# A state-space layer with a routed mixture of experts: VectorE's up product and its second scan change places

## What is computed

```python
xz = rms_norm(x) @ in_proj_w ; xb, z = split(xz)
xc = silu(causal_conv4(xb) + conv_b)
dt, B, C = split(xc @ x_proj_w)
dt = softplus(dt @ dt_proj_w + dt_proj_b)
h[t] = exp(dt[t] * A) * h[t-1] + dt[t] * B[t] * xc[t]     # 512 channels x 16 states
y[t] = sum_s h[t, :, s] * C[t, s]
out = ((y + xc * D) * silu(z)) @ out_proj_w + x
...
g = x @ gate_proj[e] ; u = x @ up_proj[e]                 # for all 16 experts e
y = sum_e combine[:, e] * ((silu(g) * u) @ down_proj[e])  # combine: 4 chosen of 16, else 0
```

## Time and profile before

| | |
|---|---|
| median of three runs | 2569.0 us (2568.81 to 2570.22) |
| the profiled execution, its own time | 2567.86 us |
| its span, first to last instruction | 2566.1 us |
| granted TensorE clock, mean | 0.972 |
| TensorE busy | 2358.2 us, 92% |
| VectorE busy | 2383.7 us, 93% |
| ScalarE busy | 1624.6 us, 63% |
| GpSimd busy | 1507.3 us, 59% |
| scans (line 1140), 2 x 512 | 626.5 + 595.0 us, mean 1262 and 1203 ns |
| gate product, up product (lines 1230, 1235), 256 each | mean 676 and 663 ns |

### The profile page before, as it was taken

The page is one execution under the profiler, slowest core; times in us unless marked ns, Lnnn a source line. Parts: engine busy times, 40 slices in busy tenths (PEclk is TensorE's granted clock), DMA queues, the critical chain, the costliest instruction groups (busy, mean ns, idle before and its releaser), DMA issues.

```text
span 2566.1 us, 26884 instructions
## 1 busy us (share of the span) xinstructions
PE 2358.2 (92%) x8416; PEld 1173.7 (46%) x8416; DVE 2383.7 (93%) x3057; ACT 1624.6 (63%) x3266; POOL 1507.3 (59%) x531
## 2 busy tenths in 40 slices
PE   6556899999999999999999999999999999988998
PEld 2112354544545454454545445454544545443555
DVE  4999999999999999999999999999999999999642
ACT  6565667676766667676676757667676766655341
POOL 0554566656566666666666566666657566666522
PEclk9767899999999999999999999999999999999999
DMA  4441443545254453525345353534535353443232
GB/s 140 179 148 41 150 142 121 170 117 186 80 169 140 131 178 113 181 90 166 131 132 189 101 181 102 166 128 132 181 100 187 112 158 119 143 158 93 77 77 64
DMA packets 172922, 344.51 MB, mean 134 GB/s; under 512 B 16075, under 2 KB 81388, under 8 KB 164460
## 3 DMA queue, kind: packets, MB, share of 16 engines
q1 hardware_dynamic: 164860, 334.93, 39.4%
q0 software_dynamic: 7920, 7.87, 2.3%
HBM read 291.35 MB, written 51.38 MB: 134 GB/s over the span
## 4 chain that ended last, share of the span: by engine, by line
DVE 59%; issue 18%; PE 12%; ACT 10%; DMA 0%; POOL 0%; DVEq 0%; ACTq 0%; POOLq 0%
DVE hs L1140 27%; DVE hs L1118 14%; DVE th L1235 5%; DVE th L1230 5%; PE Gp L494 3%; ACT dA L605 3%; PE MY L512 3%; PE FP L419 3%; DVE XC L1068 2%; PE Up L502 2%; DVE SZ L1147 1%; ACT SZ L678 1%; ACT L605 1%; PE Y L528 1%; ACT L678 1%
## 5 line engine op out<-in xcount | busy, mean ns | idle before, releaser
L963 POOL TENSOR_TENSOR hs<-hs,Cb 128x2048 f32<-128x2048 f32 x256 | 1160.7, 4534 | 169.4 <-DVE hs L1118 168.8
L605 ACT ACTIVATE dA<-dtr,A 128x512 f32<-128x512 f32 x1024 | 701.4, 691 | 678.2 <-DVE hs L1140 675.7
L948 POOL TENSOR_TENSOR th<-th,cmb 128x512 f32<-128x512 f32 x256 | 337.4, 1321 | 873.1 <-DVE hs L1118 775.9
L1140 DVE TENSOR_TENSOR_SCAN hs<-dA,carry,hs 128x512 f32<-128x512 f32 x512 | 626.5, 1262 | 6.2 <-ACT dA L605 6.0
L1118 DVE TENSOR_TENSOR hs<-dxr,Bb 128x2048 f32<-128x2048 f32 (+3 forms) x483 | 616.9, 1280 | 1.8 <-PE Y L528 1.8
L1140 DVE TENSOR_TENSOR_SCAN hs<-dA,hs 128x512 f32<-128x512 f32 x512 | 595.0, 1203 | 15.1 <-ACT dA L605 14.6
L494 PE MATMUL Gp<-x2T,Wgu 128*128 128x512 f32 x1024 | 507.7, 618 | 41.2 <-DVE th L1230 39.7
L512 PE MATMUL MY<-Wdn,th 128*128 128x256 f32 x2048 | 486.0, 381 | 0.8 <-POOL th L948 0.8
L502 PE MATMUL Up<-x2T,Wgu 128*128 128x512 f32 x1024 | 483.2, 594 | 0.0
L512 PEld LDWEIGHTS MY<-Wdn,th 128*128 128x128 f32 x2048 | 383.3, 190 | 136.3 <-issue 92.4
L494 PEld LDWEIGHTS Gp<-x2T,Wgu 128*128 128x128 f32 x1024 | 175.6, 190 | 365.4 <-issue 278.0
(11 more groups left out here) (189 smaller groups left out, 1795.6 us busy)
## 6 DMA issues: line engine op xcount, KB each, us to landing
dxr<-dx_d SPq DMA_DIRECT2D x128, 512.0 KB, 7.2
cmb<-cm_d SPq DMA_DIRECT2D x256, 256.0 KB, 3.7
dtr<-dt_d SPq DMA_DIRECT2D x63, 1024.0 KB, 5.5
Wdn<-in_w_dn SPq DMA_DIRECT2D x256, 128.0 KB, 3.6
Bb<-bc_d SPq DMA_DIRECT2D x64, 256.0 KB, 3.0
Cb<-bc_d SPq DMA_DIRECT2D x64, 256.0 KB, 3.5
dt_d<-XB SPq DMA_DIRECT2D x15, 1024.0 KB, 4.3
dx_d<-DX SPq DMA_DIRECT2D x15, 1024.0 KB, 5.9
```

What stands on the lines that cost most here:

```text
L605: act.activation(dA[h % 2][:, :], dtr[:, M % 2, beta, :], ACT.Exp, scale=A[:, k:k + 1]).then_inc(s_dA, 1)
L948: pool.tensor_tensor(th[:, q % NTH, :], th[:, q % NTH, :], cmb[:, q % 2, :], ALU.mult).then_inc(m_a, 1)
L963: pool.tensor_tensor(hs[:, G % NH, :, :], hs[:, G % NH, :, :], Cb[:, s, :].unsqueeze(1).broadcast_to([P, NBETA, CH]), ALU.mult).then_inc(s ...
L1140: dve.tensor_tensor_scan(hv, dA[h % 2][:, :], hv, first, ALU.mult, ALU.add).then_inc(s_h, 1)
```

## The change

VectorE issues `scan(G, 1)` ahead of `expert_up` of the group's first expert, in every group that has both. In groups with two experts the second one's gate and up stay where they are. The computation on `ties` at the start is removed with its semaphore, and A is multiplied by the constant -1.0.

```diff
@@ prepare
                 dve.memset(picked[:, :, NE:], 1e-20)
                 dve.memset(top8[:, 1, :, :], TAKEN)
-                ties = comb[:, 16:64]
-                dve.memset(ties[:, 0:16], 3.0)
-                dve.memset(ties[:, 32:48], 8.0).then_inc(t_dve, 1)
-                dve.wait_ge(t_dve, 1)
...
-                dve.match_replace(ties[:, 16:32], top8[:, :, 0, 0:TOPK], ties[:, 0:16], TAKEN).then_inc(t_dve, 1)
-                dve.wait_ge(t_dve, 4)
-                dve.scalar_tensor_tensor(out=ties[:, 16:32], in0=ties[:, 16:32], scalar=TAKEN, in1=ties[:, 32:48], op0=ALU.is_equal, op1=ALU.mult).then_inc(t_dve, 1)
-                dve.wait_ge(t_dve, 5)
-                dve.tensor_reduce(ties[:, 0:1], ties[:, 16:32], AX.X, ALU.add).then_inc(t_dve, 1)
-                dve.wait_ge(t_dve, 6)
-                dve.tensor_scalar(ties[:, 1:2], ties[:, 0:1], -1.0, None, ALU.mult).then_inc(t_dve, 1)
-                dve.wait_ge(t_dve, 7)
                 dve.memset(XB[:, :, 0:HIST], 0.0).then_inc(w_dve, 1)
                 dve.wait_ge(w_act, 1)
-                dve.tensor_scalar(A[:, :], A[:, :], ties[:, 1:2], None, ALU.mult).then_inc(w_dve, 1)
+                dve.tensor_scalar(A[:, :], A[:, :], -1.0, None, ALU.mult).then_inc(w_dve, 1)
@@ the loop over groups, VectorE
                 if S:
                     scan(G, 0)
+                if S:
+                    scan(G, 1)
                 if done:
                     expert_up(done[0])
                 if S:
-                    scan(G, 1)
                     scan(G, 2)
                 if len(done) == 2:
                     expert_gate(done[1])
```

More of the change, by code:

```diff
@@ L209, in sandwich_kernel @@
         dt_0, dx_0, st_dt0, st_dx0, ld_half, s_u0 = (sem(k) for k in ('dt_0', 'dx_0', 'st_dt0', 'st_dx0', 'ld_half', 's_u0'))
-        x1_sum, out_sum, z_add, m_half, z_last, t_dve = (sem(k) for k in ('x1_sum', 'out_sum', 'z_add', 'm_half', 'z_last', 't_dve'))
+        x1_sum, out_sum, z_add, m_half, z_last = (sem(k) for k in ('x1_sum', 'out_sum', 'z_add', 'm_half', 'z_last'))
         block = ctx.enter_context(nc.Block())
```

## The result

| | before | after |
|---|---|---|
| median of 14 runs each, side by side | 2569.16 us (2568.14 to 2570.22) | 2574.66 us (2573.81 to 2576.31) |
| ratio, 95% interval | | 1.0022 [1.0015, 1.0030] |
| span of the profiled execution | 2566.1 us | 2572.4 us |
| granted TensorE clock, mean | 0.972 | 0.973 |
| VectorE busy / TensorE busy | 2383.7 / 2358.2 us | 2384.8 / 2368.1 us |

The change makes the kernel slower by 5.5 us. The forecast was +2.4 with "within 0.2%" (5.1 us) as the likeliest case; the time lies inside the forecast range, just past those 0.2% on the slow side.

What follows compares the result with a forecast made beforehand. The prediction took VectorE's work and waits to bound the middle and TensorE the end. Its terms, -8.3 + 5.9 + 2.0 + 2.8 = +2.4 us on 2569.0, gave 2571.4 us, range 2563.0 to 2578.0.

Steps and rivals of the forecast that it cites:

- Group 4, the gain: In group 4 VectorE's wait for n_v shrinks as the second scan ends 0.58 us earlier: 14 chunks x 0.59, -8.3 us.
- Group 13, through group 11: Group 11's later up matmul delays z2, tanh and the decay before group 13's third scan: 13 x 0.45, +5.9 us.
- Group 9, through group 7: Group 7's later up matmul brings a new wait before group 9's third scan: 6 x 0.34, +2.0 us.
- Group 5: TensorE 0.1 to 0.35 us later in groups 14 to 0, taken as absorbed, at worst 0.1 in every second chunk.
- The end: From about 2365 us, three two-expert groups start the second up matmul some 1.15 us later each: +2.8 us after gaps.
- The test products: Removing them at the start costs and gains zero, since VectorE then idles 4.88 us waiting for ScalarE.
- A: Rival: TensorE's delay is absorbed in the middle, -8.3 and the end's +2.8 stand: 2563.5 us, chance 0.15.
- B: Rival: group 11's delay passes on whole, group 13's wait grows by 1.18 instead of 0.45: 2580.9 us, chance 0.15.
- C: Rival: TensorE's clock falls behind the added pauses, +13.8 us over 13 chunks: 2585 us, chance 0.04.
- D: Rival: nothing moves, ScalarE's and TensorE's shifts cancel within 1 us: 2569 us, chance 0.04.

Runs made afterwards that it cites:

- undoing of group 11: The changed kernel with the old order kept in group 11 only: 2571.15 us, ratio 1.0008 to the kernel before.
- double dose: The changed kernel, but in group 11 the up product comes one scan later still, behind the third scan: 2594.99 us, ratio 1.0103 to the kernel before.
- the exchange alone: The changed kernel with the test products kept, the new order everywhere: 2575.16 us, ratio 1.0022 to the kernel before.
- the first filling: New order only in groups 3 and 4; in group 13 half of the next group's inputs ahead of the third scan: 2623.35 us, ratio 1.0212 to before.
- the removal alone: The kernel before with only the computation on ties (test products) removed, the old order everywhere: 2568.19 us, ratio 0.9996.
- group 4 alone: The changed kernel with the new order only in group 4, the old one elsewhere: 2562.36 us, ratio 0.9966 to the kernel before.
- all but group 7: The changed kernel with the old order kept in group 7 only: 2571.88 us, ratio 1.0012 to the kernel before.

## Why the prediction was right and where it failed

**Group 4, the gain.** Forecast 14 x 0.59 = 8.3; measured 7.90 in the 13 chunks of the middle, right link by link: in even chunks 0.12 us of the wait for n_v is left, where 0.15 was forecast. In chunk 15 the 0.7 us are there too, but by another wait and so by luck: VectorE's wait for n_v fell only from 0.70 to 0.52 us, and 0.62 us came ahead of group 4, whose gate product waited 0.29 instead of 0.91 us for tanh.

**Group 13, through group 11.** Forecast 13 x 0.45 = 5.9; measured 4.42, 0.34 per chunk. The mechanism is right, the size 0.1 too large. z2 came 0.46 us later, as forecast. What I missed is small: behind its idle time z2 took 1.98 us, without one 1.88, so 0.1 came back before tanh (0.36 later). The undoing of group 11 and the double dose show both sides of the term: 0.34 for the first, all of 1.15 for the second.

**Group 9, through group 7.** Forecast 6 x 0.34 = 2.0; measured 2.99. The wait is 0.34 us to the digit, but a wait costs more than its length: VectorE's next instruction usually starts 0.08 us before the one ahead of it ends, and a wait loses that overlap too. Per event the ledger shows 0.45; likewise 0.76 for the 0.65 in group 5. The odd chunks added 0.05 each.

**Group 5: the step that failed.** The prediction's "in groups 14 to 0 TensorE gets 0.1 to 0.35 us later, which I see absorbed, or at worst 0.1 per chunk in every second chunk" was wrong: it cost 0.76 us in each even chunk, 5.4 us, and this is the whole difference between "no change that can be told" and a slowdown. Two errors made it. I looked for TensorE's delay alone, and the place where the two engines meet had 0.36 us of room, which 0.40 us would barely have touched. But my own gain in group 4 moves VectorE 0.6 us towards TensorE at that same place. I followed the gain up to n_v and no further. Of the 5.4 us, keeping the old order in groups 14 to 0 takes 3.0 away; the other 2.5 stay as long as group 4 gains.

**The end.** Forecast +2.8. The stretch from chunk 15 to the end is +2.14; 0.73 us were gained in its groups 3 and 4, so the two-expert groups cost 2.87 (ledger of groups 11 to 14: -0.31, +1.07, +0.87, +1.18; the exchange alone repeats each within 0.01). No fall of the clock lay in these groups, neither before nor after. The rows, which answer to the earlier trace rows:

```profile
2393.73 1.89 PE L494 MATMUL Gp<-x2T,Wgu 128*128 128x512 f32 x4
2396.66 1.98 PE L502 MATMUL Up<-x2T,Wgu 128*128 128x512 f32 x4 [1.05 <-DVE th L1215]
...
2409.42 1.98 PE L502 MATMUL Up<-x2T,Wgu 128*128 128x512 f32 x4 [0.97 <-DVE th L1215]
```

In each of the three groups that the forecast named one up matmul idles about 1 us (the third, at 2374.04 us, 0.97), and TensorE sets the time there.

**The test products.** Forecast zero; measured by themselves 0.02 us at the first scan.

**The sum.** Terms as measured from chunk 2 on: -8.6 + 4.4 + 3.0 + 5.4 + 2.9 and 0.4 of small entries = 7.5, the 5.37 + 2.14 of the ledger. The profiled execution was 1.1 us ahead at chunk 2, which no edit explains (next section). The medians are 5.5 us apart.

**The rivals.** A (all absorbed): the waits contradict it. B (group 11's delay passes whole): group 13 grew by 0.34, far from 0.65; it is right only for a second dose. C (the clock): the granted clock stayed at 1.00 in the middle with pauses of up to 1.2 us, so "by these rows I add nothing" held. The rule weighed against it (the Trainium skill, page "TensorE: Matmul & The Clock Gate", part 1: a TensorE that was idle gets half its clock) does act in this kernel, but it was seen only behind longer pauses: 2.14 us in the double dose, 3.6 us in the first filling. D (nothing moves): +5.5 rules it out.

## What to carry to other kernels

A gain on one engine is a delay of every other engine against it. Follow it past the wait that it removes to the next place where the two meet, and look up the room there, which no list of waits shows: it is the distance between the end of the one and the start of the other. And where an edit stands in a loop over unlike groups, apply it only in the group where it pays: here one group of sixteen gave -7 us, all sixteen +5.5.

## What was not expected of the hardware

- **A VectorE product stood still for GpSimd, the instructions around it did not.** Beside `read_out` the product of two SBUF tensors waited until GpSimd's end (3.56 us for 1.21). In the same rows the scan at 1067.46 kept its 1.21 us with `read_out` running since 1066.54, and so did the product with Up its 0.66. Each of these two reads one input from PSUM (dA, Up) and only one from SBUF, so the page named above, which speaks of two SBUF inputs, agrees with them as well. A scan with both inputs in SBUF was not run.
- **Behind which of TensorE's pauses the clock fell.** From 290 to 2300 us, with the clock at 1.00 ahead of the pause: behind none of the 58 pauses of 0.5 to 1.2 us in the changed kernel, nor behind any in the kernel before, the longest 1.6 us; at 1.96 us (double dose) in none of 7; at 2.14 us in 2 of 6 (2.4 to 1.2 GHz for 3.4 us); at 2.81 us, once in the first filling, it fell; at 3.60 to 3.75 us in 12 of 13, for 3.4 or 6.8 us (the one at 315.60 us was spared).
- **The start is not repeatable, the middle is.** From chunk 2 to chunk 15 the ledger repeats within 0.15 us between profiles of the same order (two pairs: the changed kernel and the exchange alone, 0.02; the kernel before and the removal alone, 0.15). The way to chunk 2, where the granted clock alternates, does not: three versions with the same start as others (the exchange alone, group 4 alone, all but group 7) were 4.5 to 4.8 us ahead of before at chunk 2 in their profiled executions, the others lay between 2.1 ahead and 1.4 behind. The kernel before itself has single runs of 2563.93 and 2564.35 us beside a median of 2569.86. In chunk 15 a fall of the clock inside group 11 (at 2356.4 to 2373.2 us, in four of the variants' profiles) cost 1.2 us each time. What decides this was not tried. So here a term of 1 to 3 us is read from the ledger of the middle, not from the medians.
